# A macaron block with two expert stages: 159 blocks for 160, gathers issued in front of scatters, and the block table made behind the row statistics

## The reference

```python
x = x + 0.5 * ffn(layernorm(x), gate, up, down, topk_idx, topk_weight)
x = x + attention(layernorm(x), Wqkv, b_qkv, Wout, b_out)
x = x + 0.5 * ffn(layernorm(x), gate, up, down, topk_idx, topk_weight)
# ffn: 32 experts, top 4; per token and chosen expert
#   o = (silu(x @ gate.T) * (x @ up.T)) @ down.T * weight, summed over the four
#   widths 512 -> 256 -> 512, all in float32
```

## Time and profile before

| | |
|---|---|
| median of three runs | 2656.75 us (2655.46 to 2657.82) |
| profiled execution: its own time, span | 2657.12 us, 2655.3 us |
| routing, to the first instruction of f1 | 0 to 96.2 us |
| f1, to the issue of its last scatter | 96.2 to 888.6 us |
| attention, to the first instruction of f2 on POOL | to 1854.8 us |
| f2 | 1854.8 to 2655.3 us |
| busy: PE, ACT, POOL, DVE | 2405.6, 1517.3, 1338.9, 1324.6 us |
| mean granted clock of PE | 0.957 |

### The profile page before, as it was taken

The page is one execution under the profiler, slowest core; times in us unless marked ns, Lnnn a source line. Parts: engine busy times, 40 slices in busy tenths (PEclk is TensorE's granted clock), DMA queues, the critical chain, the costliest instruction groups (busy, mean ns, idle before and its releaser), DMA issues. The chain is left out here.

```text
span 2655.3 us, 66428 instructions
## 1 busy us (share of the span) xinstructions
PE 2405.6 (91%) x12341; PEld 1823.5 (69%) x12342; DVE 1324.6 (50%) x3662; ACT 1517.3 (57%) x3779; POOL 1338.9 (50%) x1296
## 2 busy tenths in 40 slices
PE   0599999999999569999999999996899999999998
PEld 0488888888888445665656656553788888888886
DVE  8545555555533335546455454552455555555432
ACT  4666666666655325445454454542666666666654
POOL 4155655565555214444454444534465555666554
PEclk9899999999999779999999999986899999999999
DMA  8677877788720223333333343331678777878500
GB/s 302 195 185 171 180 182 173 179 189 191 176 26 0 79 73 84 96 104 102 109 89 97 95 108 99 89 97 39 176 177 198 173 171 176 193 176 196 110 0 1
DMA packets 181206, 348.83 MB, mean 131 GB/s; under 512 B 47143, under 2 KB 98215, under 8 KB 179986
## 3 DMA queue, kind: packets, MB, share of 16 engines
q0 software_dynamic: 76416, 148.62, 27.2%
q1 hardware_dynamic: 93456, 189.91, 24.6%
q10 hardware_dynamic: 11266, 9.61, 1.3%
HBM read 228.24 MB, written 117.96 MB: 130 GB/s over the span
## 5 line engine op out<-in xcount | busy, mean ns | idle before, releaser
L559 PE MATMUL f_psg<-f_wh,f_xh 128*128 x1280 | 534.4, 418 | 5.8 <-DVE f_idle L720 5.4
L559 PE MATMUL f_psg<-f_wh,f_xl 128*128 x1280 | 504.2, 394 | 0.0
L559 PE MATMUL f_psg<-f_wl,f_xh 128*128 x1280 | 501.5, 392 | 0.0
L507 POOL DMA_INDIRECT f_xg<-xn_rows,f_it x320 | 353.4, 1104 | 117.5 <-issue 93.2
L515 POOL DMA_INDIRECT x_rows<-f_ob,f_it x160 | 255.0, 1594 | 293.9 <-ACT f_ob L656 144.6
L515 POOL DMA_INDIRECT out<-f_ob,f_it x160 | 256.7, 1604 | 284.1 <-ACT f_ob L656 123.6
L1403 DVE CUSTOM_DVE_ANT_0 a_psa<-a_psa,cst 128x384 f32<-128x384 f32 (+3 forms) x512 | 247.3, 503 | 250.6 <-PE a_psa L1121 247.7
L656 ACT ACTIVATE f_ob<-f_pso,f_wcol 128x512 f32<-128x512 f32 x320 | 220.8, 690 | 192.3 <-issue 136.9
L1019 POOL TENSOR_TENSOR a_pt<-a_pt 128x256 f32<-128x256 f32 (+2 forms) x384 | 267.2, 734 | 120.6 <-PE a_psc L1149 114.0
L1276 ACT ACTIVATE a_pt<-a_psb 128x256 f32<-128x256 f32 (+3 forms) x512 | 213.7, 438 | 198.6 <-PE a_psb L1184 193.7
L727 DVE TENSOR_TENSOR f_xl<-f_psx,f_xh 128x512 fp32r<-128x512 f32 x320 | 221.4, 692 | 134.5 <-ACT f_xh L637 88.2
(11 more groups left out here) (194 smaller groups left out, 4325.0 us busy)
## 6 DMA issues: line engine op xcount, KB each, us to landing
f_wraw<-w_in SPq DMA_DIRECT2D x128, 768.0 KB
a_stq<-a_qk SPq DMA_DIRECT2D x128, 144.0 KB
a_stk<-a_qk SPq DMA_DIRECT2D x128, 144.0 KB
r_xt<-x_in SPq DMA_DIRECT2D x8, 1024.0 KB, 14.3
xn_rows<-r_xt SPq DMA_DIRECT2D x8, 1024.0 KB, 15.2
a_xt<-x_rows SPq DMA_DIRECT2D x8, 1024.0 KB, 5.3
a_x<-x_rows SPq DMA_DIRECT2D x8, 1024.0 KB, 5.4
out<-a_x POOLq DMA_DIRECT2D x8, 1024.0 KB, 4.9
```

What stands on the lines that cost most here:

```text
L507: g.indirect_dma_start(xg[:, n % XB, :], None, xn_d, bass.IndirectOffsetOnAxis(it[:, n:n + 1], 0), bounds_check=tok_max, oob_is_err=False) ...
L559: mm = pe.matmul(psg[:, j, :], x[:, j, k, :], w[:, cols], start=(k == 0 and n == 0), stop=(k == DC - 1 and n == 2))
```

## The change

Three edits. `NU = (NP + E * (P - 1)) // P` = 159 is the largest number of blocks that any routing can use; both expert stages run 159 blocks and no longer `NB` = 160 (the tables keep their width). POOL issues the gather of block b in front of the scatter of block b-6, not behind it; its loop covers blocks 16 to 143, and the 15 blocks behind it are written out. In routing, DVE's 12 instructions for the block table stand directly behind the statistics of the second half of the rows, in front of the product over 128x4096, with their wait for `s_blk`.

```diff
+NU = (NP + E * (P - 1)) // P
...
                     v.tensor_scalar(inv[:, ts], st[:, ts, 7], EPS, None, ALU.add).then_inc(s_mom, 1)
 
-                v.wait_ge(s_at, E)
-                ch.step(v.tensor_tensor(at[:, :, :], at[:, :, :], onehot[:, :, :], ALU.mult))
...
-                    v.tensor_tensor(eqc[:, h, :, :, :], matched(1, js, NB), numbered(NB), ALU.is_equal).then_inc(s_eqc, 1)
-
-
                 v.wait_ge(s_blk, 1)
                 blk = tb["blk"]
                 ch.step(v.tensor_scalar(bt_i[:, :], cst_r[0:1, C_ROW - C_KEEP:C_ROW - C_KEEP + NB + 2],
...
                 ch.step(v.scalar_tensor_tensor(blk[:, 3, :], bt[:, 0, :], 16.0, bt[:, 2, :], ALU.mult, ALU.add))
+
+                v.wait_ge(s_at, E)
+                ch.step(v.tensor_tensor(at[:, :, :], at[:, :, :], onehot[:, :, :], ALU.mult))
...
+                    v.tensor_tensor(eqc[:, h, :, :, :], matched(1, js, NB), numbered(NB), ALU.is_equal).then_inc(s_eqc, 1)
 
                 v.wait_ge(s_mm, NCH)
...
-            with eng.Fori(1, NB // NS - 1) as i:
+            with eng.Fori(1, (NU - 1) // NS) as i:
...
-            for b in range(NB - NS, NB):
+            for b in range((NU - 1) // NS * NS, NU):
                 turn(b, b % NS)
...
                 for b in range(IB):
                     if b % XB == 0:
                         fetched = indices(b, b, b // XB)
+                    gather(b, b, fetched)
                     if b >= LAG:
                         scatter(b - LAG, b - LAG)
-                    gather(b, b, fetched)
-                with g.Fori(1, NB // IB) as i:
+                with g.Fori(1, NU // IB) as i:
                     for n in range(IB):
                         b = i * IB + n
                         if n % XB == 0:
                             fetched = indices(b, n, i * (IB // XB) + n // XB)
+                        gather(b, n, fetched)
                         scatter(b - LAG, (n + IB - LAG) % IB)
-                        gather(b, n, fetched)
-                for b in range(NB - LAG, NB):
+                for b in range(NU // IB * IB, NU):
+                    if b % XB == 0:
+                        fetched = indices(b, b % IB, b // XB)
+                    gather(b, b % IB, fetched)
+                    scatter(b - LAG, (b - LAG) % IB)
+                for b in range(NU - LAG, NU):
                     scatter(b, b % IB)
...
-                turn_h(NB - 1, 1)
-                down(NB - 1, 1, (NB - 1) % NS)
+                turn_h(NU - 1, (NU - 1) % 2)
+                down(NU - 1, (NU - 1) % 2, (NU - 1) % NS)
```

More of the change, by code:

```diff
@@ L234, in _ @@
                     v.tensor_scalar(inv[:, ts], st[:, ts, 7], EPS, None, ALU.add).then_inc(s_mom, 1)
+                v.wait_ge(s_blk, 1)
+                blk = tb["blk"]
+                ch.step(v.tensor_scalar(bt_i[:, :], cst_r[0:1, C_ROW - C_KEEP:C_ROW - C_KEEP + NB + 2],
+                                        float(OB - 1), None, ALU.add))
+                ch.step(v.tensor_scalar(bt_i[:, :], bt_i[:, :], 2, None, ALU.arith_shift_right))
+                ch.step(v.tensor_scalar(bt[:, 2, :], bt_i[:, :], 16.0, -16.0, ALU.mult, ALU.add))
+                ch.step(v.tensor_scalar(blk[:, 0, :], ps_blk[:, 0:NB + 2], float(E - 1), None, ALU.min))
+                ch.step(v.tensor_tensor(bt[:, 0, 1:NB + 2], blk[:, 0, 1:NB + 2], blk[:, 0, 0:NB + 1],
+                                        ALU.not_equal))
+                ch.step(v.tensor_tensor_scan(bt[:, 1, :], bt[:, 0, :], bt[:, 0, :], 2.0, ALU.add, ALU.max))
+                ch.step(v.tensor_copy(bt_i[:, :], bt[:, 1, :]))
+                ch.step(v.tensor_scalar(bt_i[:, :], bt_i[:, :], NS - 1, None, ALU.bitwise_and))
+                ch.step(v.tensor_copy(bt[:, 1, :], bt_i[:, :]))
+                ch.step(v.tensor_scalar(blk[:, 2, :], bt[:, 1, :], float(WROW), float(SLOT0), ALU.mult, ALU.add))
+                ch.step(v.tensor_tensor(blk[:, 1, :], bt[:, 0, :], blk[:, 2, :], ALU.mult))
+                ch.step(v.scalar_tensor_tensor(blk[:, 3, :], bt[:, 0, :], 16.0, bt[:, 2, :], ALU.mult, ALU.add))
                 v.wait_ge(s_at, E)
@@ L264, in _ @@
                     v.tensor_tensor(eqc[:, h, :, :, :], matched(1, js, NB), numbered(NB), ALU.is_equal).then_inc(s_eqc, 1)
[L267 to L282, removed]
                 v.wait_ge(s_mm, NCH)
@@ L422, in blocks @@
                 turn(b, b)
-            with eng.Fori(1, NB // NS - 1) as i:
+            with eng.Fori(1, (NU - 1) // NS) as i:
                 for r in range(NS):
                     turn(i * NS + r, r)
-            for b in range(NB - NS, NB):
+            for b in range((NU - 1) // NS * NS, NU):
                 turn(b, b % NS)
-        there = lambda b: not isinstance(b, int) or b < NB
+        there = lambda b: not isinstance(b, int) or b < NU
         with nc.Block() as block:
@@ L481, in _ @@
                     ahead(b, b % NS)
-                with sp.Fori(2, (NB - AHEAD - 1) // NS) as i:
+                with sp.Fori(2, (NU - AHEAD - 1) // NS) as i:
                     for r in range(NS):
@@ L485, in _ @@
                         ahead(i * NS + r, r)
-                for b in range((NB - AHEAD - 1) // NS * NS, NB):
+                for b in range((NU - AHEAD - 1) // NS * NS, NU):
                     go(b, b % NS)
@@ L489, in _ @@
                 for n in range(OB):
-                    sp.wait_ge(s_sca[n], 16 * (NB // OB))
+                    sp.wait_ge(s_sca[n], 16 * ((NU - n + OB - 1) // OB))
             @block.gpsimd
@@ L697, in _ @@
                 blocks(a, turn)
-                product_high(NB - 1, 1)
-                result(NB - 1, 1, (NB - 1) % XB)
+                product_high(NU - 1, (NU - 1) % 2)
+                result(NU - 1, (NU - 1) % 2, (NU - 1) % XB)
             @block.vector
@@ L768, in _ @@
                 blocks(v, turn)
-                product_low(NB - 1, 1)
+                product_low(NU - 1, (NU - 1) % 2)
 def attend(nc, tb, d):
```

## The result

The changed kernel: 2628.08 us, the median of three executions (2636.37, 2628.08, 2627.93), against 2656.75: ratio 0.990, 95% interval 0.988 to 0.992.

What follows compares the result with a forecast made beforehand. Expert stages were taken to last as long as PE's turns plus start, tail and stalls. Turns 9.66, stalls 2.58 and routing 4.9 make 17.1 us off 2656.75: 2639.6 us, range 2637 to 2646.

Steps and rivals of the forecast that it cites:

- Two turns, 9.66 us: Expert stages: 159 blocks save PE one steady turn of 4.83 us in each stage, 9.66 us.
- Two stalls, 2.58 us: Expert stages, block 10: gathers start about 5.5 us earlier, so PE's stalls of 1.53 and 1.05 us go.
- The table, 4.9 us: Routing: with the block table moved, POOL's power is no longer held; the row table starts 4.9 us earlier.
- The 1 us at the end: Routing's end: the block table delays the row table by only about 1 us behind PE's last sum.
- The power holds DVE: Routing: second table instruction waits for POOL's power; routing gives 2.0 us, not 4.9; 2642.5 us, chance 0.22.
- The product misses the last gap: Routing: POOL's product is held by DVE's long product to 59.67; only 0.75 us won; 2643.8 us, chance 0.13.
- the power misses them all: Routing: POOL's power finds no gap between DVE's instructions; routing loses 2.5 us; 2647.0 us, chance 0.03.
- Scatters behind gathers: Expert stages: gathers delay scatters waiting for their go by 1.36 us each, adding up; 2712 us in full, chance 0.03.
- My slack: Expert stages: ACT's four buffers give 19.3 us, of which 5.6 is left before scatter lag decides.
- Attention "which I take as unchanged": Attention and the two stage starts: taken as unchanged; the range goes down to 2637 for what they may give.
- the 5.3 us that I took for what the measurement can tell: Whole kernel: the measurement tells 0.2% (5.3 us) from no change; faster by more had chance 0.93.

Runs made afterwards that it cites:

- table_mid: The kernel before with the block table's 12 DVE instructions between the second and third chunk of comparisons: 2652.81 us, median of 10, ratio 0.999.
- whole: The changed kernel run again with nothing altered, for more executions: 2631.84 us, median of 6, ratio 0.991 against the kernel before.
- whole2: The changed kernel run once more with nothing altered, for size and spread: 2630.05 us, median of 6, ratio 0.989 against the kernel before.

## Why the prediction was wrong

- **Two turns, 9.66 us**: right. Still 4.83 a turn; eight turns less took 38.9 and 38.7 us.
- **Two stalls, 2.58 us**: the mechanism was right, the size wrong, and this is the step that failed in the sum: "5.5 us are more than the 1.53 and 1.05 us by which the rows were late, so both stalls go: 2.58 us". The gathers did start 5.5 us earlier against PE and no stall was left. But the stalls of that one profile were the smallest of six (3.5 to 5.2 us in the others), and I counted only PE's standing still, not the longer turn and the microseconds at 1.2 GHz behind it. Measured: 7.4 us, 4.8 more than the term.
- **The table, 4.9 us**: right in its mechanism and near in size, 4.0 to 5.0 in the profiles that have it, 4.6 on the mean. POOL's power gives nearly all of it, shown by a wait alone (4.3). The 1 us at the end comes and goes with the clock of PE's last sum, which I had taken as 1.31 us in any case; table_mid gave all of it back.
- **The power holds DVE**, the rival by the rule of whole-instruction locks: fell. The second table instruction started at 50.01, beside the running power, and took 0.28 us; its like took 0.23.
- **The product misses the last gap, or the power misses them all**: fell; the product took 0.30 and was through 0.30 us before the long product began. I had given it a margin of nothing to 0.3.
- **Scatters behind gathers**: did not happen at the lead of the changed kernel, and cost 49 us at half of it. My slack was counted at the wrong place, and its last step was off by a little (19.3 less 8.4 less 5.5 is 5.4, not 5.6).
- **Attention "which I take as unchanged"**: the other failed step. It gave the range 2.6 us of room downward, where attention took 965.1 and 959.1 us in two profiles of the changed kernel (whole, whole2), and the kernel's mean fell by 26.1 us where its terms make 21.7; the 4.4 us between lie in attention as far as is known. With it fell the 5.3 us that I took for what the measurement can tell, from three executions at 2655.5 to 2657.8, where 74 spread over 21.
- **The 28.7 us of the first result** hold some luck besides: that median lies 3.0 us below the mean of 15 executions. On the means the gain is 26.1 us: 17.1 forecast, 4.8 more from the order, 0.3 less from the table, and 4.4 that go with attention's clock, for which the cause stays open.

## What to carry to other kernels

A stall read from one profile is one draw: look for the same stall in other executions before its size goes into a sum, and add the time at the lower clock that may follow it. On a queue that is worked in order, put the operation that can run ahead in front of the one that waits, and then look at what else is queued behind the waiting one: here it was the weights behind SP's go. Where an operation on POOL takes twice its time, look at what DVE does at that moment; a wait of 3.5 us on DVE was worth 4.3 us.

## What the runs showed that I had not expected

- DVE's product with two SBUF inputs, 4.42 us long, holds a power of 16 columns on POOL until its own end: 6.96 us, against 2.92 where the product waited. Twelve short instructions of 0.23 to 0.48 us hold it not at all. The Trainium skill (SBUF — State Buffer, "Who interferes with whom") has the contention, with a lock for the whole instruction by whichever of the two comes first; the product's side of it agrees with these traces (the power ends 2.77 us after it), but the power holds no DVE instruction for its 2.9 us. What held L1370 no run here isolates.
- A stall of 2.0 to 3.1 us of PE in a stretch that it runs at 2.4 GHz was followed by a few microseconds at 1.2 GHz in seven stages of eight, which cost 1.3 to 1.6 us more than the turn behind a stall otherwise does.
- One and the same attention stage took 954.1 to 968.1 us in the profiles. In the three compared above nearly all of the difference is PE's busy time, by its granted clock. The kernel's mean moved by 8 us more than its turns with one block more or less in the stage in front of attention.
